# Eight-layer attention and feed-forward kernel on one core: both routed feed-forward layers moved into merged programs, the relu one on f16 pairs

## The reference, cut to what matters

```
x = x + L0 conv attention;            x = x + L0 quantised FFN
x = x + L1 latent attention (16 heads of 64, keys: 1024 rows of x and 77 rows of context)
x = x + L1 routed FFN (relu):
    probs = softmax(tokens @ gate_w); e = argmax(probs); pos = place of the token among those of expert e
    h = relu(token @ w1[e]); y = h @ w2[e]; out = prob * y if pos < 320 else 0
x = x + L2 cross attention (77 keys); x = x + L2 gated FFN (8 experts, all tokens)
x = x + L3 cross attention (77 keys, a bias of its own per head)
x = x + L3 routed FFN (gelu, with b1 and b2, no limit on the number of tokens of an expert)
```

## Time and profile before

| | us |
|---|---|
| median of 3 runs | 3333.82 |
| lowest and highest of them | 3331.04 and 3334.6 |
| the profiled execution's own time | 3337.32 |
| its span, first to last instruction | 3335.7 |
| mean granted clock of TensorE | 0.916 of full speed |

### The profile page before, as it was taken

The page is one execution under the profiler, slowest core; times in us unless marked ns, Lnnn a source line. Parts: engine busy times, 40 slices in busy tenths (PEclk is TensorE's granted clock), DMA queues, the critical chain, the costliest instruction groups (busy, mean ns, idle before and its releaser), DMA issues. The chain is left out here.

```text
span 3335.7 us, 68908 instructions
## 1 busy us (share of the span) xinstructions
PE 2891.0 (87%) x26993; PEld 1989.8 (60%) x26994; DVE 2205.5 (66%) x3297; ACT 1989.8 (60%) x2962; POOL 1338.2 (40%) x979
## 2 busy tenths in 40 slices
PE   6769998765969998969998599788999999989678
PEld 3246666424436666536666498576666666667668
DVE  5968887678868884768884222767656565558455
ACT  3448887274548885548886111566666665547357
POOL 2249998120238886128886211660000000008233
PEclk8979998887979999979999699897999999999689
DMA  4511111200022220012221610102222222145556
GB/s 141 192 61 54 56 55 57 102 13 13 1 46 55 55 54 23 1 38 57 57 56 26 233 37 30 39 10 74 77 77 76 77 76 77 51 143 138 56 197 205
DMA packets 224950, 240.63 MB, mean 72 GB/s; under 512 B 137301, under 2 KB 175234, under 8 KB 217602
## 3 DMA queue, kind: packets, MB, share of 16 engines
q1 hardware_dynamic: 210167, 184.10, 19.7%
q0 software_dynamic: 12240, 49.83, 4.3%
q10 hardware_dynamic: 2233, 2.39, 0.2%
HBM read 146.16 MB, written 52.77 MB: 60 GB/s over the span
## 5 line engine op out<-in xcount | busy, mean ns | idle before, releaser
L2669 POOL TENSOR_TENSOR lta_p_lo<-lta_p,lta_p_hi 128x1024 f16<-128x1024 f32 x256 | 538.8, 2132 | 214.5 <-DVE lta_p_hi L2792 214.5
L2864 ACT ACTIVATE lta_p<-lta_banks,lw_gmax 128x512 f32<-128x512 f32 x512 | 324.5, 684 | 109.2 <-PE lta_banks L2707 105.7
L2775 DVE TENSOR_REDUCE lta_s_ps<-lta_s_ps 128x1 f32<-128x1101 f32 x240 | 314.2, 1309 | 101.1 <-PE lta_s_ps L2685 101.1
L4446 PE MATMUL m_h_ps<-m_x,m_w 128*128 128x512 f16 x1536 | 354.5, 381 | 3.2 <-issue 3.2
L4458 PE MATMUL m_y_ps<-m_w,m_hT 128*128 128x256 f16 x3072 | 355.8, 273 | 1.3 <-DVE m_hT L4618 1.3
L4458 PEld LDWEIGHTS m_y_ps<-m_w,m_hT 128*128 128x128 f16 x3072 | 299.2, 98 | 64.3 <-issue 7.1
L4543 ACT ACTIVATE m_h<-m_h_ps,m_h_bias,m_h_scale 128x512 f32<-128x512 f32 x256 | 199.3, 779 | 231.0 <-PE m_h_ps L4446 222.8
L1244 POOL TENSOR_TENSOR c0a_tri_p_lo<-c0a_tri_p,c0a_tri_p_hi 128x1024 f16<-128x1024 f32 (+2 forms) x192 | 285.7, 1522 | 60.1 <-DVE c0a_tri_p_hi L1418 59.0
L4618 DVE TENSOR_TENSOR m_hT<-m_h,m_hT 128x512 f16<-128x512 f32 x256 | 176.3, 692 | 200.7 <-ACT m_hT L4543 197.0
L4446 PEld LDWEIGHTS m_h_ps<-m_x,m_w 128*128 128x128 f16 x1536 | 150.9, 98 | 160.7 <-issue 7.4
L1493 ACT ACTIVATE c0a_tri_p<-c0a_banks,c_size 128x512 f32<-128x512 f32 (+3 forms) x384 | 209.1, 578 | 47.0 <-PE c0a_banks L1312 35.2
(11 more groups left out here) (818 smaller groups left out, 6590.1 us busy)
## 6 DMA issues: line engine op xcount, KB each, us to landing
m_w<-pw_w SPq DMA_DIRECT2D x23, 1024.0 KB
m_w<-in_L_ffn_w_dram SPq DMA_DIRECT2D x2, 8192.0 KB
m_raw<-in_L_ffn_W_dram SPq DMA_DIRECT2D x16, 1024.0 KB, 6.6
pwo_raw<-in_L_ffn_w_dram POOLq DMA_DIRECT2D x16, 1024.0 KB, 8.1
pw_w<-pwo_pair POOLq DMA_DIRECT2D x16, 1024.0 KB, 4.4
lta_q<-ltb_qT SPq DMA_DIRECT2D x96, 128.0 KB, 2.4
c_side<-in_fside_Bx16xSxS_dram SPq DMA_DIRECT2D x16, 616.0 KB, 4.8
c0a_tri_q<-c_near SPq DMA_DIRECT2D x96, 96.0 KB
```

The costliest lines, as they stand in the source:

```text
L2669: nc.gpsimd.tensor_tensor(p_lo[:, slot, :], p32[:, p32_slot(h, j), :], p_hi[:, slot, :], ALU.subtract).then_inc(rested, 1)
L2775: nc.vector.tensor_reduce(ntop_of(h)[:, n:n + 1], scores(h, n), AX_X, ALU.max, negate=True).then_inc(top_ready, 1)
L2864: nc.scalar.activation(p32[0:rows, slot, c * 512:(c + 1) * 512], t_ps[0:rows, c, :], ACT.Exp, bias=bias, scale=p["gmax"][0:rows, 0:1]).the ...
L4446: last = nc.tensor.matmul(h_ps[:, f % RING, :], w1[:, v, a, c, f * P:(f + 1) * P], x16[:, b, c, n * CHUNK:(n + 1) * CHUNK], start=c == 0 a ...
```

## The change

- A new class `RoutedPairs` makes f16 pairs of L1's w1 and w2 (16 pieces of 1 MB). In `latent_project` of each batch ACT takes the sum of absolute values of eight pieces (`Abs`, 128x2048). In `latent_attend` of the second batch each head h has piece h: SP stores piece h-2 and loads piece h, ACT makes two high halves (`halve`, 128x1024) and DVE two low ones (`split`, 128x1024, two inputs in SBUF).
- The emit block of the second batch, the norm, the gates and the routing of L1 become one block (`emit_and_route`). It makes a table `ids` with the place of 320 tokens at most kept by a factor, as L3's does, and stores x and normed rows as table rows; w1's pairs (8 MB) are loaded beside it into SBUF that held keys and values. `sorted_x`, its zeros and the 16 scatters are gone.
- `relu_experts_stage` replaces `routed_experts`: f16 pairs, rows gathered by `ids`, w2 in a ring of three, x + weight*y scattered straight back as rows of x. c2 loads them with four DMAs of 512 KB ahead of its wk, wv and wq, instead of the 16 gathers and `complete`.
- L3: c3o, m3r and m3e become one block (`projected_routed_stage`), the gate weights are loaded first, and the transpositions and gate products of tile t-9 stand behind the projection of tile t.

```diff
+        held = ExitStack()
         with ExitStack() as kept:
             latent = LatentWeights(nc, env, kept, args, "L1_xattn")
             quant_ffn_stage(nc, env, "qf", quant, latent)
-            latent_attention_stage(nc, env, "lt", args, "L1_xattn", latent)
-        slot, weight = ctx.enter_context(nc.sbuf_tensor("slot", [P, TILES], U32)), ctx.enter_context(nc.sbuf_tensor("weight", [P, TILES], F32))
-        sorted_y = routed_ffn_stage(nc, env, "m1", args, "L1_ffn", ACT.Relu, False, 320, slot, weight)
-        cross_attention_stage(nc, env, "c2", args, "L2_xattn", rows(args["mask_Bx1xSxS2_bk1"]), None, 1, (sorted_y, slot, weight))
+            routed = RoutedPairs(nc, env, held, args, "L1_ffn", latent.room)
+            latent_attention_stage(nc, env, "lt", args, "L1_xattn", latent, lambda n: args[f"L1_ffn_{n}"], routed)
+        relu_experts_stage(nc, env, "m1", routed)
+        held.close()
+        cross_attention_stage(nc, env, "c2", args, "L2_xattn", rows(args["mask_Bx1xSxS2_bk1"]), None, 1, routed.x_rows[1:T + 1, :])
         pairs = PairWeights(nc, ctx, args, "L3_ffn")
         gated_ffn_stage(nc, env, "m2", args, "L2_ffn", pairs)
         pairs.hold(ctx)
-        cross_attention_stage(nc, env, "c3", args, "L3_xattn", rows(args["mask_Bx1xSxS2_ik1"]), args["fside_Bx16xSxS2_0"], 0, routed=pairs)
-        paired_routed_stage(nc, env, "m3", "L3_ffn", args, ACT.Gelu, None, pairs, out.rearrange("b s d -> (b s) d"))
+        attended = ctx.enter_context(nc.sbuf_tensor("attended", [P, TILES, D], F32))
+        cross_attention_stage(nc, env, "c3", args, "L3_xattn", rows(args["mask_Bx1xSxS2_ik1"]), args["fside_Bx16xSxS2_0"], 0, routed=pairs,
+                              into=attended)
+        projected_routed_stage(nc, env, "m3", "L3_ffn", args, attended, args["L3_xattn_Wo"], args["L3_xattn_bo"], ACT.Gelu, pairs,
+                               out.rearrange("b s d -> (b s) d"))
...
+            if 1 <= s <= MINE:
+                i = s - 1
+                act.wait_ge(piece_loaded[i % 2], 16 * (i // 2 + 1))
+                nc.scalar.activation(pieces[:, i % 2, :], pieces[:, i % 2, :], ACT.Abs,
+                                     accum_out=routed.size[:, MINE * b + i:MINE * b + i + 1]).then_inc(measured, 1)
...
+            if routed is not None:
+                if h >= 2:
+                    routed.store(sp, h - 2)
+                routed.load_again(sp, h)
...
+                if routed is not None and j in (TURN, LAST):
+                    routed.split(dve, h, j // LAST)
...
+                if routed is not None and j in (0, LAST - 1):
+                    routed.halve(act, h, j // (LAST - 1))
...
+    def load_again(self, sp, k):
+        if k >= 2:
+            sp.wait_ge(self.split_done, 2 * (k - 1))
+        self.load(sp, k, self.raw(k), self.raw_loaded[k % 2])
+
+    def store(self, sp, k):
+        sp.wait_ge(self.split_done, 2 * (k + 1))
+        sp.dma_start(self.dram[k % 2][k // 2], self.pair(k)).then_inc(self.stored[k % 2], 16)
...
+    def halve(self, act, k, part):
+        if part == 0:
+            act.wait_ge(self.raw_loaded[k % 2], 16 * (k // 2 + 1))
+            if k == 0:
+                act.wait_ge(self.linked, RoutedPairs.LINKS)
+            if k >= 2:
+                act.wait_ge(self.stored[k % 2], 16 * (k // 2))
+        self.nc.scalar.activation(self.part(k, 0, part), self.raw_part(k, part), ACT.Identity,
+                                  scale=self.down[:, k:k + 1]).then_inc(self.halved, 1)
+
+    def split(self, dve, k, part):
+        dve.wait_ge(self.halved, 2 * k + part + 1)
+        self.nc.vector.scalar_tensor_tensor(self.part(k, 1, part), self.raw_part(k, part), self.down[:, k:k + 1], self.part(k, 0, part),
+                                            ALU.mult, ALU.subtract).then_inc(self.split_done, 1)
...
+    BESIDE = {0: (0, 1), 1: (2, 3), 2: (4, 5), 3: (6, 7), 6: (8, 9), 7: (10, 11)}
+    LATE = range(12, TILES)
...
+        sp.dma_start(wo16[:], p["wo"]).then_inc(wo_loaded, 16)
+        sp.dma_start(bout[:], w("bout").partition_broadcast(P)).then_inc(loaded, 16)
+        sp.dma_start(gate[:], ffn("gate_w").rearrange("(c p) e -> p c e", p=P)).then_inc(gate_loaded, 16)
...
+        sp.wait_ge(routed.stored[0], 16 * E)
+        store_x(0)
+        store_x(1)
+        for g in range(2):
+            for e in range(4 * g, 4 * g + 4):
+                load_w1(e)
+            store_rows(g)
...
+        sp.wait_ge(routed.stored[1], 16 * E)
+        for g in range(2, 4):
+            store_x(g)
+            store_rows(g)
...
-def routed_experts(nc, env, st, ctx, func, sorted_x, sorted_y, expert_of, w1, w2, b1, b2, weights_loaded):
...
+        with nc.Block() as block:
+            project_rows(nc, env, Stage(nc, ctx, tag + "p"), block, w, weight, bias, r)
+            route_rows(nc, env, Stage(nc, ctx, tag + "r"), block, w, None,
+                       ((pairs.h_scale, r["h_in"]), (pairs.h_down, r["h_down"]), (pairs.y_scale, r["y_back"])), r, pairs)
+            paired_experts(nc, env, Stage(nc, ctx, tag + "e"), block, func, pairs, r, out)
...
+    GROUPS, BEHIND = TILES // CHUNK, 9
...
+        store_x(0)
+        for g in range(1, GROUPS):
+            store_x(g)
+            store_rows(g - 1)
+        store_rows(GROUPS - 1)
...
+            project(t)
+            look(t - BEHIND)
+        for t in range(TILES - BEHIND, TILES + 2):
+            look(t)
...
+            for j in range(NT):
+                if j >= W2_RING:
+                    sp.wait_ge(y_done, j - W2_RING + 1)
+                load_reduction(nc, sp, routed, r, j)
...
+                for f in range(FC):
+                    for c in range(DC):
+                        for m, (a, b) in enumerate(PAIRS_OF_HALVES):
+                            last = nc.tensor.matmul(h_ps[:, u, f * P:(f + 1) * P], w1[:, u, a, c, f * P:(f + 1) * P], x16[:, u, b, c, :],
+                                                    start=c == 0 and m == 0, stop=c == DC - 1 and m == 2)
...
+                nc.vector.tensor_copy(w1[:, u].rearrange("p a c f -> p (a c f)"), routed.w1[:, bass.ds(e, 1), :].rearrange("p a n -> p (a n)")
...
+        if combine is not None:
+            for g in range(groups):
+                sp.dma_start(env.x[:, g * CHUNK:(g + 1) * CHUNK, :],
+                             combine[g * CHUNK * P:(g + 1) * CHUNK * P, :].rearrange("(t p) d -> p t d", p=P)).then_inc(x_loaded[g], 16)
...
-        def complete(t):
-            dve.wait_ge(gathered[t], 16)
-            nc.vector.scalar_tensor_tensor(env.x[:, t, :], yg[:, t, :], weight[:, t:t + 1], env.x[:, t, :], ALU.mult,
-                                           ALU.add).then_inc(added, 1)
```

More of the change, by code:

```diff
@@ L3274 @@
+        add(TPB - 1)
+        for n in range(TPB - 2, TPB):
+            sum_row(n)
+        spread_of(2)
+        invert(2)
+        normalise(range(FIRST + 4, TILES))
+        for m in range(2):
+            dve.wait_ge(routed.stored[m], 16 * E)
 class PairWeights:
@@ L3606, in _ @@
+        for table, out in tables:
             tt(product[:], mine[:], table[:].unsqueeze(1).to_broadcast([P, NT, E]), ALU.mult)
             reduce(out[:], product[:], ALU.add)
-def paired_experts(nc, env, st, ctx, func, pairs, r, out):
+        if capacity is not None:
+            tt(product[:], mine[:], starts[:].unsqueeze(1).to_broadcast([P, NT, E]), ALU.mult)
+            reduce(fill[:], product[:], ALU.add)
+            ts(used[:], tile_ids[:], float(P), lane1[:, 0:1], ALU.mult, ALU.add)
+            tt(used[:], used[:], fill[:], ALU.subtract)
+            ts(used[:], used[:], capacity + 1.5, None, ALU.is_lt)
+            tt(r["y_back"][:], r["y_back"][:], used[:], ALU.mult)
@@ L3612, in paired_experts @@
+def paired_experts(nc, env, st, block, func, pairs, r, out):
     sb, ps, sem = st.sb, st.ps, st.sem
```

934 lines of the change are left out of this document (566 added, 368 removed).

## The result

The changed kernel takes 3321.16 us in the median of 19 runs (3314.46 to 3329.67), the kernel before 3333.25 (3328.12 to 3340.40) beside it: a ratio of 0.9966 with a 95% interval of 0.9959 to 0.9972, 12 us less. The forecast was 3279 with a range up to 3314. The sign was right, three quarters of the gain are missing. The profiled execution has a span of 3317.5 us at a clock of 0.919.

The account below looks back on a forecast made before the run. PE was taken as the bound in attend block and relu experts, with holes around both routings. Terms -40 - 15 + 3 - 3 - 30 + 6 + 24 = -55 gave 3282, less 3.5 for the median: 3279 us, range 3243 to 3314.

Parts of the forecast that it names:

- Relu experts, -40: L1's relu expert stage: 23 tiles at L3's f16-pair pace instead of f32, 40 us less.
- they don't reach L3's pace: Rival for the relu experts: 6.3 us a tile instead of 5.5, 18 us more, 3297 us; chance 0.09.
- Table rows, "100 GB/s, so 4.2 MB in 42 us": Row stores in both merged blocks: 4.2 MB at 100 GB/s take 42 us, ending together with the ids.
- the DMAs end last: Rival for both merged blocks: rows at 73 GB/s take 57 us, each 15 us later, 3309 us; chance 0.14.
- PE waiting for table rows rather than for `ids`: Recorded sign, in the profile after, that the prediction would be wrong; no size given.
- L1's emission, norm and routing, -15: L1's merged block: first expansion at about 1892 to 1893 instead of 1907.8, 15 us less, bounds -25 to 0.
- the forecast's signs (1893 and 30): Relu stage's first expansion expected near 1893 plus the 30 us that projection and attend lost.
- L3 in one block, -30: L3's merged projection, routing and experts: first expansion at 3165.5 instead of 3195.7, 30 us less, bounds -20 to -33.
- Attend block, +24: Second batch's attend block: new passes cost 13 us, DVE and POOL contention 11, 24 us more, bounds 0 to 74.
- projection, +6: Latent projection: the Abs passes on ACT put 0.4 us of each of 16 on the path, 6 us more.
- the attend block hides it: Rival: PE bounds a head, so the 24 and the 6 us fall away, 3249 us; chance 0.19.
- c2, -3: Start of c2: query products quicker and `complete` gone, but x loads stand ahead of wk; 3 us less, bounds 0 to -6.

Follow-up runs that it names:

- rows_528: The changed kernel with table rows of 528 words instead of 513, tables left in place, weight written as 64-byte pieces: 3262.52 us, ratio 0.9802.
- tables_first: The changed kernel with its two row tables declared as the first DRAM tensors, all instructions and bytes the same: 3259.06 us, ratio 0.9788.
- before_first: The kernel before the change with its one row table declared as the first DRAM tensor, all instructions the same: 3322.89 us, ratio 0.9982.
- blocks_528: rows_528 with L3's routed stage in three blocks again, as in the kernel before: 3271.22 us, ratio 0.9824.
- attend_bare: The changed kernel with halve and split cut to one column from the second batch's third head on: 3297.04 us, ratio 0.9899.
- aligned: The changed kernel with rows of 528 words, both tables declared as the first DRAM tensors, padding zeroed once early: 3262.97 us, ratio 0.9804.
- touched: The changed kernel with the tables left in place and their last column written once early: 3331.89 us, ratio 1.0008.

## Why the prediction was wrong, point by point

The span by its landmarks, in us, before, after, and in rows_528, where the stores are quick; the forecast is the difference to before.

| from, to | before | forecast | after | rows_528 |
|---|---|---|---|---|
| start, first q product of the projection | 840.6 | 0 | 836.5 | 835.7 |
| to the first emitted product, second batch | 978.5 | +30 | 988.3 | 985.0 |
| to L1's first expansion | 88.7 | -15 | 100.2 | 70.7 |
| to its last expansion | 163.1 | -40 | 123.5 | 123.8 |
| to c2's first score | 57.2 | 0 | 57.2 | 55.4 |
| to c3's first score | 873.6 | 0 | 872.0 | 874.1 |
| to L3's first expansion | 194.0 | -30 | 199.2 | 172.3 |
| to the end | 140.0 | 0 | 140.6 | 142.0 |
| span | 3335.7 | -55 | 3317.5 | 3259.0 |

- **Relu experts, -40.** Right: -39.6 after, -39.3 in rows_528. The rival in which they don't reach L3's pace is out.
- **Table rows, "100 GB/s, so 4.2 MB in 42 us".** This is the step that failed. I made a rate out of 73 GB/s and a share of 0.86, and took the 21.2 us of the earlier trace rows as a sign of full queues; then "two ends meet". The queues were full because the pieces were slow to be written (share 0.91 at 95 GB/s, against 0.46 at 141 for the same stores in tables_first): 1 KB pieces in a table of that width at that place. The stores end up to 30 us behind the ids in both merged blocks. The merges bring the ids forward and leave the stores no such room as before, and the weight's 4-byte pieces are the last in the queue. It is the rival "the DMAs end last" in kind; it put 15 us on each block, and the gathers came 24.5 and 29 us further behind the ids than forecast. The sum had 42 us for the rows; in L3 they took 64, from the first store's issue at 3090.5 to the last landing at 3154.7, and the weight's 8 KB store, for which it had no term at all, landed 13 us later. The kernel before could have told both: its rows of L3 took 49.6 us (3114.7 to 3164.3), and the weight's store another 11, until 1.1 us ahead of the ids. The recorded sign of being wrong, PE waiting for table rows rather than for `ids`, is the one that came.
- **L1's emission, norm and routing, -15.** With quick stores the path is 18 us shorter, so the products and the routing were costed well; with the slow ones it is 11.5 us longer. That L1's experts start at 1925.0, close to the 1923 of the forecast's signs (1893 and 30), is luck: slow stores (+29.5) stood against a cheaper attend block and projection (-20), an earlier start (-4) and a shorter rest of the path (-3).
- **L3 in one block, -30.** Mis-sized apart from the stores: 22 us less in rows_528. Of it 10.3 come from quick stores alone (before_first) and 11.2 from the merge (blocks_528 against rows_528), so the term of 30 was for the most part no price of the blocks: the 194.0 us it was taken from already held slow stores. From wo's first product to the last gate I forecast 31 us; 38 were measured. From gates to ids it is 16.0, as costed, and from ids to expansion 11.9 in rows_528 where I put 10.9.
- **Attend block, +24, and projection, +6.** Too dear. The 16 `Abs` passes of 1.91 us cost nothing: the projection and the first attend block together take as long as before. A head pays 0.28 us instead of 1.5. The whole stretch pays 4 to 10 us in the kernels with this code, and the second attend block alone, from its first score to the first emitted product, 8 to 10 (374.9 us against 365.0). Of these, 4.3 are in the heads and 5.6 come behind the last head's start, where no next head follows; attend_bare gives back 8.4. So the rival "the attend block hides it" was nearer than the forecast. The contention is in the rows: `split` takes 1725 ns in the median, 2497 at most, against 1273 at least, and POOL's pass 3127 at most. 17 of the 32 splits lie beside a POOL pass for their whole length, and they are the ones of 1725 ns and more; the others take 1273 to 1277. The Trainium skill (SBUF — State Buffer, Who interferes with whom) says that a VectorE instruction with two inputs in SBUF and a GpSimd one that reads SBUF contend for one port, which the one locks against the other. The trace agrees in that both grow, but in no split by a whole POOL pass of 2.13 us. DVE is busy 327 of 392 us and POOL 288, so there is room, and PE is the bound. I had costed a hole that is too small for a pass as lost path; work that another engine isn't yet waiting for just moves into the next hole.
- **c2, -3, and the scatter's tail, +3.** Right together, 0 after and -2 in rows_528.
- **The start, 0.** 4.1 us less. c0 no longer writes the zeros of `sorted_x`, but that this is the cause isn't shown: before_first still writes them and has 837.7 us, inside the 835.7 to 838.8 of the kernels without.

In spans the forecast was -55 and the result -18, 37 us apart: slow stores +56 (100.2 - 70.7 and 199.2 - 172.3), L3's merge and its stores in the kernel before +8, projection and attend block -20, the start -4, L1's path -3. The 56 hang on one execution: in others with the same code at the old place the two paths were as short as 89.3 and 192.3 us, which makes the slow stores 39 to 56. The median of the runs lies 2 us above the profiled execution's own time; that of the kernel before lay 4 below its own, so the medians are only 12 us apart.

## What to carry to other kernels

Before a merge or an overlap, look at how long the stores take to land and not only at what the trace names as the end of a wait: a store that lands 1 us ahead of it today becomes the last event of the merged block. 512 KB in 21 us beside a DMA share of 0.86 and a rate of 73 GB/s is a sign of dear pieces and not of many bytes, and two cheap tests showed it here: pad the row (2052 to 2112 bytes), or declare the table at another place. And price passes on an engine with idle time by the room it has in a whole head, not hole by hole, and the last head by itself.

The best versions here, tables_first and rows_528, stand at 3259 and 3263 us, 2.1 and 2.0% under the kernel before. rows_528 is the one to keep, since 528-word rows were quick at both places tried (aligned has the other, 3263 us).

## What was not expected of the hardware

- The same instructions on the same bytes, with only the DRAM tables declared elsewhere: 512 KB in 1 KB pieces land in 4.6 us or 23.7, and 8 KB in 4-byte pieces in 8.9 or 42.4. With 528-word rows at the slow place it is 2.9.
- It is not the width alone (513 words declared first are quick), nor the place alone (528 words at the old place are quick), nor a first write (touched). What about the place matters stays open. Both original places are slow, those with 1 MB more declared ahead less so, the first declared quick, and no row shows the memory behind the DMA engines.
- Slow stores and other traffic do more than add up: L1's path is 76.8 us with the slow place alone, 71.8 with w1's loads alone, and 89.3 to 100.2 with both.
